# Attention block: tokens split into two f16 parts in natural layout and turned by transposing DMAs

## The reference

```python
h = jnp.maximum(_layernorm(x, axis=-1), 0.0)
q, k, v = (split_heads(h @ W.T) for W in (Wq, Wk, Wv))
a = jnp.einsum('bhnd,bhmd->bhnm', q, k) * D ** (-0.5) + (adj + adj)[:, None]
p = jax.nn.softmax(jnp.where(jnp.any(a != 0, -1, keepdims=True), a, -jnp.inf), -1)   # NaN -> 0
out = x + jnp.einsum('bhnm,bhmd->bhnd', p, v).transpose(0, 2, 1, 3).reshape(B, N, D) @ Wo.T
```

## Time and profile before

| | |
|---|---|
| median of 3 runs | 1287.07 us (1287.06 to 1287.58) |
| the profiled execution | 1287.33 us, of which the span from first to last instruction is 1285.5 us |
| mean granted clock of TensorE | 0.995 of full speed |
| busy share of the span | PE 97%, PEld 86%, DVE 87%, ACT 82%, POOL 69% |
| transfers | 163.88 MB, the DMA engines busy 48.9% of the time on SP's queue |

### The profile page before, as it was taken

How to read it: one execution, slowest core, us unless ns; L and a number is a source line. 1 busy time by engine, 2 the same in 40 slices (tenths; PEclk the granted TensorE clock), 3 DMA queues, 4 the chain that set the end, 5 groups by cost and what they waited for, 6 DMA issues and landing times. The chain is left out here.

```text
span 1285.5 us, 43965 instructions
## 1 busy us (share of the span) xinstructions
PE 1245.4 (97%) x13104; PEld 1109.5 (86%) x13104; DVE 1114.6 (87%) x4006; ACT 1054.7 (82%) x2427; POOL 884.3 (69%) x1262
## 2 busy tenths in 40 slices
PE   4899999999999999999999999999999999999996
PEld 4788988888988888988888988888988888888885
DVE  6798889888889898889898889898889898888884
ACT  4788888888888888888888888888888888888885
POOL 1676677776677776777776777776777766777765
PEclk9999999999999999999999999999999999999999
DMA  6344554554544554554554544554544554544541
GB/s 228 84 108 119 143 122 118 143 131 116 145 122 116 145 130 114 147 122 115 147 129 114 149 121 114 148 127 114 151 119 114 150 125 115 152 118 114 135 116 57
DMA packets 90772, 163.88 MB, mean 127 GB/s; under 512 B 14976, under 2 KB 23168, under 8 KB 90752
## 3 DMA queue, kind: packets, MB, share of 16 engines
q1 hardware_dynamic: 90752, 163.64, 48.9%
HBM read 46.14 MB, written 16.78 MB: 49 GB/s over the span
## 5 line engine op out<-in xcount | busy, mean ns | idle before, releaser
L884 POOL TENSOR_TENSOR fold<-minus 128x512 f32<-128x512 f32 x256 | 327.4, 1279 | 293.6 <-DVE bounds L739 293.5
L567 ACT ACTIVATE probs<-minus,bounds 128x256 f32<-128x256 f32 x1024 | 459.5, 498 | 23.8 <-DVE bounds L739 23.8
L748 DVE TENSOR_TENSOR pT_lo<-pT_ps,pT_hi 128x512 f16<-128x512 f32 x512 | 351.3, 686 | 62.5 <-ACT pT_hi L578 59.3
L578 ACT ACTIVATE pT_hi<-pT_ps 128x512 f16<-128x512 f32 x512 | 304.9, 595 | 109.7 <-PE pT_ps L403 108.1
L739 DVE CUSTOM_DVE_ANT_0 minus<-s_ps,adj_now 128x256 f32<-128x256 f32 x1024 | 388.5, 416 | 5.9 <-ACT probs L567 4.7
L403 PE MATMUL pT_ps<-ident,probs 128*128 128x128 f32 x2048 | 307.6, 273 | 1.8 <-ACT probs L567 1.6
L328 PE MATMUL job_ps<-hT_hi,w_hi 128*128 128x256 f16 x1024 | 280.2, 274 | 1.4 <-DVE w_lo L689 0.9
L328 PE MATMUL job_ps<-hT_hi,w_lo 128*128 128x256 f16 x1024 | 279.0, 272 | 0.0
L328 PE MATMUL job_ps<-hT_lo,w_hi 128*128 128x256 f16 x1024 | 278.8, 272 | 0.0
L403 PEld LDWEIGHTS pT_ps<-ident,probs 128*128 128x128 f32 x2048 | 241.8, 140 | 19.4 <-ACT probs L567 3.0
L392 PE MATMUL s_ps<-qk_stack 96*128 96x256 f32 x1024 | 246.4, 323 | 0.7 <-DVE w_lo L689 0.7
(11 more groups left out here) (77 smaller groups left out, 2253.0 us busy)
## 6 DMA issues: line engine op xcount, KB each, us to landing
qk_stack<-qk_parts SPq DMA_DIRECT2D x768, 128.0 KB, 2.3
x_in<-x SPq DMA_DIRECT2D x32, 512.0 KB, 3.4
x_res<-x SPq DMA_DIRECT2D x32, 512.0 KB, 3.7
out<-y SPq DMA_DIRECT2D x64, 256.0 KB, 2.1
adj_in<-adj SPq DMA_DIRECT2D x32, 256.0 KB, 3.5
w_in<-wq SPq DMA_DIRECT2D x2, 512.0 KB, 6.7
w_in<-wk SPq DMA_DIRECT2D x2, 512.0 KB, 8.2
w_in<-wv SPq DMA_DIRECT2D x2, 512.0 KB, 7.9
```

The source lines that it names most:

```text
L567: end = nc.scalar.activation(probs[hh % 2][:, t, :], minus[hh // 2 % 2][:, hh % 2, t, :], ACT.Exp, bias=bounds[:, hh // 2 % 4, 2 * (hh % 2 ...
L578: nc.scalar.activation(pT_hi[hh % 4][:, :, :], pT_ps[hh % 2][:, :].rearrange("p (m n) -> p m n", m=NT), ACT.Copy).then_inc(pT_high, 1)
L748: nc.vector.tensor_tensor(pT_lo[hh % 4][:, :, :], pT_ps[hh % 2][:, :].rearrange("p (m n) -> p m n", m=NT), pT_hi[hh % 4][:, :, :], ALU.sub ...
L884: nc.gpsimd.tensor_tensor(f1[:, :, :], src[:, :, 0:N // 2], src[:, :, N // 2:N], ALU.add).then_inc(folded1, 1)
```

## The change

- The job "h" goes, with its eight transposes a batch, its PSUM bank turns and its evacuations L529 and L703. `JOBS` spreads the remaining pieces anew over heads 0, 1 and 4 to 13.
- POOL's `h` is now the relu of x minus the mean, without the factor `rstd`. ACT writes the high f16 part, scaled by `rstd`, into `h_parts` (`split_tokens`, two instructions), DVE the low part (`low_tokens`, two), both SBUF to SBUF and with tokens still on partitions.
- Two `dma_start_transpose` a batch on SP's queue, one for each token tile (128 x 1024 f16, 256 KB), turn `h_parts` into `hT`. PE waits for both before qk 0.
- Moments, normalisation and split of a batch lie one batch earlier: in batch b, for batch b + 2, moments at the end of head 6, normalisation at POOL's head 7, the split at head 10. The turn for batch b + 1 is issued in batch b.

```diff
-    4: [("h", 0, 1, 0, 4), ("y", 0, -1, 0, 6)],
-    5: [("y", 0, -1, 6, 9), ("h", 1, 1, 0, 4), ("y", 0, -1, 9, 12)],
-    6: [("qk", 0, 1, 0, 12)],
+    4: [("y", 0, -1, 0, 6)],
+    5: [("y", 0, -1, 6, 12)],
+    6: [("qk", 0, 1, 0, 13)],
     ...
+            def turn_tokens(b, t, first):
+                sp.wait_ge(h_split, b + 1)
+                ...
+                if not first:
+                    sp.wait_ge(ended["v"], count("v", 2 + t, b - 1))
+                    settled(sp, "sp")
+                sp.dma_start_transpose(hT[:, t, :, :], h_parts[:, t, :, :].rearrange("p a d -> p (a d)")
+                                       ).then_inc(h_turned[t], 16)
             for i, half in TURNS:                                   # prologue
                 sp.dma_start(w_in[i]...).then_inc(w_loaded[i][half], 16)
+                if (i, half) == (WV, 0):
+                    for t in range(NT):
+                        turn_tokens(0, t, True)
                 stack(1, b, first)                                  # SP's body
-                if not (last or isinstance(b, int) and b + 2 == B):
-                    load_tokens(b + 2)
+                if not last:
+                    turn_tokens(b + 1, 0, False)
+                    if not (isinstance(b, int) and b + 2 == B):
+                        load_tokens(b + 2)
+                    turn_tokens(b + 1, 1, False)
                     if n == 0 and start == 0:                       # PE, job "qk"
-                        pe.wait_ge(taken["h"], count("h", 0, b + d))
+                        for turned in h_turned:
+                            pe.wait_ge(turned, (b + (d + 1)) * 16)
-                                          [lambda k, v=v: v[:, k, :] for v in hT], ...
+                                          [lambda k, a=a: hT[:, :, a * KT + k, :] for a in range(2)], ...
+            def split_tokens(b, first):                             # ACT
+                act.wait_ge(h_ready, b + 1)
+                ...
+                for t in range(NT):
+                    end = nc.scalar.activation(h_parts[:, t, 0, :], h[:, t, :], ACT.Copy, scale=rstd[:, t:t + 1])
+                end.then_inc(h_high, 1)
+                    if not (nearly or last) and hh == 10:           # before high_probs(b, hh)
+                        split_tokens(b + 2, False)
+            def low_tokens(b):                                      # DVE
+                dve.wait_ge(h_high, b + 1)
+                for t in range(NT):
+                    end = nc.vector.scalar_tensor_tensor(h_parts[:, t, 1, :], h[:, t, :], rstd[:, t:t + 1],
+                                                         h_parts[:, t, 0, :], ALU.mult, ALU.subtract)
+                end.then_inc(h_split, 1)
-                    if not last and hh == 0:
-                        moments_of(b + 1)
+                    if not (nearly or last) and hh == 6:            # after low_probs(b, hh)
+                        moments_of(b + 2)
+                    if not (nearly or last) and hh == 10:
+                        low_tokens(b + 2)
-                    end = nc.gpsimd.tensor_scalar(h[:, t, :], x_in[:, t, :], minus_mean[:, t:t + 1], rstd[:, t:t + 1],
-                                                  ALU.add, ALU.mult)
+                    end = nc.gpsimd.tensor_scalar(h[:, t, :], x_in[:, t, :], minus_mean[:, t:t + 1], 0.0,
+                                                  ALU.add, ALU.max)
-                    if not last and hh == 1:                        # POOL
-                        normalise(b + 1, False)
+                    if not (nearly or last) and hh == 7:
+                        normalise(b + 2, False)
```

More of the change, by code:

```diff
@@ L185, in attention_block @@
         rstd_ready, h_ready = sem("rstd_ready"), sem("h_ready")
+        h_high, h_split = sem("h_high"), sem("h_split")
+        h_turned = [sem(f"h_turned{t}") for t in range(NT)]
         ended = {k: sem(f"ended_{k}") for k in PER_BATCH}
@@ L337, in job @@
                     begin(kind, n, d, b)
[L338 to L345, removed]
+                if kind == "qk":
                     half = PRODUCTS["qk"] // 2
                     if n == 0 and start == 0:
-                        pe.wait_ge(taken["h"], count("h", 0, b + d))
-                    if n == 0 and start <= half // 2 < stop:
-                        pe.wait_ge(taken["h"], count("h", 1, b + d))
+                        for turned in h_turned:
+                            pe.wait_ge(turned, (b + (d + 1)) * 16)
                     for i, w in enumerate((WQ, WK)):
                         if start < (i + 1) * half and stop > i * half:
-                            end = product(ps[:, i * N:(i + 1) * N],
+                            end = product(ps[:, i * N:(i + 1) * N].rearrange("p (t n) -> p t n", t=NT),
                                           [lambda k, w=m: w[:, k, n * P:(n + 1) * P] for m in (w_hi[w], w_lo[w])],
-                                          [lambda k, v=v: v[:, k, :] for v in hT], start - i * half, stop - i * half)
+                                          [lambda k, a=a: hT[:, :, a * KT + k, :] for a in range(2)],
+                                          start - i * half, stop - i * half)
                 elif kind == "v":
                     t, half = n % NT, n // NT
-                    end = product(ps[:, 0:HALF], [lambda k, v=v: v[:, k, t * P:(t + 1) * P] for v in hT],
+                    end = product(ps[:, 0:HALF], [lambda k, a=a: hT[:, t, a * KT + k, :] for a in range(2)],
                                   [lambda k, w=w: w[:, k, half * HALF:(half + 1) * HALF] for w in (w_hi[WV], w_lo[WV])],
@@ L548, in take @@
                     nc.scalar.activation(y[:, n, :], ps[:, :], ACT.Copy).then_inc(taken["y"], 1)
+            def split_tokens(b, first):
+                act.wait_ge(h_ready, b + 1)
+                if not first:
+                    for turned in h_turned:
+                        act.wait_ge(turned, b * 16)
+                for t in range(NT):
+                    end = nc.scalar.activation(h_parts[:, t, 0, :], h[:, t, :], ACT.Copy, scale=rstd[:, t:t + 1])
+                end.then_inc(h_high, 1)
             def copy_outputs(b, pair, early):
@@ L590, in _ @@
             scale_weight(WK, 0)
-            for n in range(2):
-                take("h", n, 0)
+            split_tokens(0, True)
             high_weight(WQ, 0)
@@ L612, in _, with body @@
             exponentials(0, 0, True)
-            def body(b, first, last):
+            def body(b, first, nearly, last):
                 for hh in range(HEADS):
@@ L627, in body @@
                         take(kind, n, b + d, first and (kind, d) in (("v", 0), ("qk", 0)))
+                    if first and hh == 3:
+                        split_tokens(1, False)
+                    if not (nearly or last) and hh == 10:
+                        split_tokens(b + 2, False)
                     if hh == HEADS - 3 and not last:
@@ L630, in body @@
                     high_probs(b, hh, first and hh < 4)
[L632 to L635, removed]
+            body(0, True, False, False)
+            with act.Fori(1, B - 2) as b:
+                body(b, False, False, False)
+            body(B - 2, False, True, False)
+            body(B - 1, False, False, True)
             copy_outputs(B - 1, PAIRS - 1, False)
@@ L775, in _ @@
             weight_scales(WK, 0)
-            for n in range(2):
-                take("h", n, 0)
+            low_tokens(0)
             low_weight(WQ, 0)
@@ L814, in body @@
                     low_probs(b, hh, first and hh < 2)
-                    if not last and hh == 0:
-                        moments_of(b + 1)
[L818 to L821, removed]
+                    if first and hh == 0:
+                        moments_of(1)
+                    if first and hh == 3:
+                        low_tokens(1)
+                    if not (nearly or last) and hh == 6:
+                        moments_of(b + 2)
+                    if not (nearly or last) and hh == 10:
+                        low_tokens(b + 2)
+            body(0, True, False, False)
+            with dve.Fori(1, B - 2) as b:
+                body(b, False, False, False)
+            body(B - 2, False, True, False)
+            body(B - 1, False, False, True)
             any_nonzero(B - 1, PAIRS - 1)
@@ L927, in body @@
                             divide(b - 1, PAIRS - 1)
-                    if not last and hh == 1:
-                        normalise(b + 1, False)
+                    if first and hh == 1:
+                        normalise(1, False)
+                    if not (nearly or last) and hh == 7:
+                        normalise(b + 2, False)
                     for kind, n, d in ended_before(hh, first, last):
@@ L932, in body @@
                             residual(b + d, n)
[L934 to L937, removed]
+            body(0, True, False, False)
+            with pool.Fori(1, B - 2) as b:
```

(3 more changed lines are left out.)

16 lines of the change are left out of this document (7 added, 9 removed), and 18 rows, old and new, of the table JOBS.

## The result

The changed kernel takes 1532.14 us (median of 4 runs, 1528.9 to 1536.71) against 1287.3 before: ratio 1.1904, 95% interval 1.1872 to 1.1937. It is slower by 245 us; the forecast was 1460, its range 1380 to 1640.

The account below looks back on a forecast made before the run. PE, busy 97% of the span, was taken as the bound. -0.96 - 0.33 + 5.2 + 1.0 made +4.9 us a batch, 149 together, plus 25 for the clock on 1287.3: 1460 predicted, range 1380 to 1640.

Parts of the forecast that it names:

- the sum: PE's time per batch, mainly its wait at head 6's first qk product: -0.96 - 0.33 + 5.2 + 1.0 = +4.9 us.
- The first: SP's queue: turns go at x_in's rate and issue time, PE waits 4.2 us, no clock drop; 1405 us, chance 17%.
- The second: SP's queue: turns cut small, 7.1 us each, PE waits 16.8 us; about 1855 us, 20% with all down to 1560.
- The fourth: SP's queue: twelve issues take 2.6 us, so turns and x_in land before PE comes; 1247 to 1278 us, chance 3%.
- The third: Head 6: turns come in time, DVE's moments wait 3 us a batch for x_in; 1380 us, chance 5%.
- the forecast's own case: Head 6: the second turn lands late, PE waits 5.2 us a batch; 1460 us, own range 1420 to 1560, chance 55%.
- the bound of 74 for all: PE's clock after the head 6 stalls: upper bound of 74 us if all 31 drop it; 25 us was taken.
- +1.0: Heads 10 to 12: uncovered split work on ACT and DVE ends on PE, 1.0 us a batch, bounds 0.4 and 2.5.
- -0.33: Head 2: PE's wait of 0.33 us a batch was to go as the moments move away from head 0.
- The saving: PE's stream: the eight transposes a batch go, taking 0.60 and 0.36 us, 0.96 us together.
- POOL at nothing: POOL's normalisation as add and max in place of add and multiply: costed at nothing, in a gap POOL has.

Follow-up runs that it names:

- the run with all three: Changed kernel with x_in loaded first and turns among the second stack, POOL's add and multiply, and moments, normalisation, split one head earlier: 1289.97 us, ratio 1.0017.
- The run with x_in early: Changed kernel with only SP's queue reordered: x_in's load ahead of the second stack, both turns still behind it; 1477.2 us, ratio 1.1474.
- the filled wait: Changed kernel with 52 unread matmuls on PE ahead of its wait for the turns, not in batch 0; 1549.26 us, ratio 1.2037.

## Why the prediction held, and where it did not

**The place and sign were right.** PE idles at its first qk product of head 6, ended by the second turn, with bn_stats waiting for x_in beside it; SP's stacks keep 7.7 us. In the batch shown PE arrives 8.8 us after the stack's first issue (614.63 to 629.04, less the wait of 5.61), where the sum had 8.9 (626.75 to 635.61). The turn's wait was 5.2 us in the sum and is 5.8 (185.0 in 32); its landing, 3.1 to 4.7 us, is near the 3 to 4.5 forecast. That the wait came out so near is in part luck: the issue was mis-sized, 1.27 us for 0.65, and the data came faster behind it, so that PE goes on 4.2 us after the second turn's issue began (624.87 to 629.04), where the sum had 4.4.

**The rivals.** The first (1405) had a wait of 4.2 us, and fell; its lower bound, by its own terms, is 1388 and not 1380. The second (packets of 256 bytes at 7.1 us a turn) had the small packets and not their price: 1040 more under 512 bytes come with each turn (82560 against 16000 with plain copies, over 64), and it lands in 3.3 us. The fourth (quick issues) fell: the twelve take 7.71 us. The third is taken up next.

**What the sum did not see: the waits beside PE's.** The sum follows PE alone, and as an account of where PE's time goes it holds. As an account of what costs the time it does not: with PE's wait for the turn gone the kernel took 1539 us. The third rival let DVE's moments wait only "after all", if the turns came in time, for 93 us. They wait in the forecast's own case, 4.0 us a batch, and without the turn's wait x_in's lateness was worth 104 us (1539 to 1435), near the rival's price. The other 147 us stood in no term: neither the sum nor a rival had POOL's normalisation at head 7, with ACT's split behind it, as a wait. With the queue's two waits gone, its old form gave 127 of them back and its earlier place 141.

**The clock.** I let every third stall drop it, 25 us. PE's busy time in ten batches is 14.2 us longer though 5.4 went (the 0.54 a batch of the run with all three): 19.7 us, or 2.0 a batch and 61 in 31, near the bound of 74 for all. The first rival took a stall of 4.2 us as too short to drop it. The run with x_in early is against that, by the row that ends PE's wait of 4.07 us and the window behind it, at the lower level of the clock:

```profile
605.12 0.58 PE L355 MATMUL job_ps<-hT,w_hi 128*128 128x256 f16 x2 [4.07 <-DMA hT<-h_parts]
```

```profile
605.10:608.00 2.90, 2.88 (x14) 2.11 (x15) 0.00 (x0) 0.00 (x0) 2.48 (x7) 0.50 0.00 0
```

In the changed kernel's own trace the loss adds to the sum, since PE's busy and idle time make up the span; it is not what a faster clock would give back, as the filled wait showed.

**From 1460 to 1532.** In the ten batches of the windows above PE's wait for the turn is this:

```profile
PE job_ps L347 <- DMA hT<-h_parts: 60.1, 10, 6.3
```

A batch grew by 7.8 us and not by 4.9 and 0.8 for the clock, 2.1 more: the clock costs 1.2 more, the turn's wait 0.8 (6.0 for 5.2), the saving is 0.4 smaller, and PE's other idle time grew by 0.4 where +1.0 and -0.33 made 0.7. In thirty batches that is 63 us. Up to the same issue of the third adjacency load, which moved from 77.17 to 91.45 us, 14 us came against some 5 forecast (1 in the prologue, 3.9 in the first batch): 9. Together they come to the 72, in rounded terms; the last batches were not traced.

**The saving.** I took 0.96 us for eight transposes from where rows start and end. PE's busy time shows 0.54 net of all that changed on it, in the run with all three, whose window is at full clock like the one before. The 0.33 us that I took off for head 2 was the weight loader's wait; all of PE's idle time before is 0.20 us a batch.

**Heads 10 to 12, and POOL at nothing.** PE's idle time besides the turn's wait is 0.6 us a batch (6.58 less 6.0) against 0.2 before, so the 1.0 us on PE is 0.4 at most in the changed kernel. The split's durations, which I kept for sources in SBUF, are 0.72 and 0.76 us for 0.589 and 0.682. POOL's new form at nothing was wrong: 2.0 us a tile, hidden behind the two queue waits (12 us), worth 127 once they are gone and the heads stay, and 6 with the heads moved (1296 to 1290). My reason, a gap on POOL, looked at POOL's load and not at ACT behind it, which stops in order.

**The page's rule.** The Trainium skill (Advanced Engine Details and Errata, X-Bar Transpose (TRN2)) has transposing DMAs as fast as regular ones; here the plain copy lands in 2.4 us and the turn in 3.3, and the queue is held 0.52 and 1.27. The measurement decides.

## What to carry to other kernels

When work moves to a DMA queue, list every engine that waits for something behind the new place, and price each wait alone and all together: removing one of several waits that run side by side can give nothing, and that is no sign that it is harmless. Ask of an operation that is moved what stands ahead of it in order on its own engine at the new place, and which in-order engine stops for it. A change that costs 19% cost 12% with another order of the queue, and 0.2% when POOL's old form and its earlier place were added, so where things stand is tried before the idea is dropped.

## What I had not expected of the hardware

- POOL's tensor_scalar on 128x512 f32 took 2002 ns as add by a pointer and max with a constant, and 773 (768 put back) as add and multiply by two pointers. Which of the two differences costs it was not tried.
- A transposing DMA holds SP's queue for 1.27 us against 0.52 for the plain copy of the same bytes, and lands in 3.3 us against 2.4.
- ACT's split from SBUF with a scale by pointer took 713 to 720 ns, with Relu and no scale 618 to 632; the evacuation from PSUM it replaced took 589.
- DVE's low part of the tokens (128x512, two sources in SBUF) took 758 ns in the changed kernel and 1088 in the run with all three. In one batch there (from 614.12 us, 2.16 us for two) POOL worked beside it, and two of its instructions took 1.05 and 0.85 us that took 0.74 and 0.41 at an earlier head of that batch. That the two engines hold each other up is a guess; it was not tried.
